# Samples dealt to the halves by twelves, count matmuls that write with a step, and a reordered prologue in a recommendation kernel

## What is computed

```python
x = _mlp(dense_x, bot, sigmoid_last=False)
pooled = jax.vmap(lambda tab, ix: jnp.take(tab, ix, axis=0).sum(axis=1))(tables, indices)
Tcat = jnp.concatenate([x[:, None, :], jnp.transpose(pooled, (1, 0, 2))], axis=1)
Z = jnp.einsum('bim,bjm->bij', Tcat, Tcat)
R = jnp.concatenate([x, Z[:, li, lj]], axis=1)      # li, lj: the lower triangle of 27 x 27
return _mlp(R, top, sigmoid_last=True)
```

## Time and profile before

| | |
|---|---|
| three runs, median (lowest to highest) | 2857.62 us (2854.86 to 2863.55) |
| profiled execution, its span | 2854.84 us, 2853.0 us |
| PE busy | 2743.9 us, 96% of the span |
| ACT busy | 2112.7 us, 74% |
| DVE busy | 1994.1 us, 70% |
| POOL busy | 1809.4 us, 63% |
| prologue, to the first sum matmul | 0 to 116 us |
| loop over the tables | 116 to about 2600 us |
| pairs of the 27 vectors and top MLP | the rest |

### The profile page before, as it was taken

How to read it: one execution, slowest core, us unless ns; L and a number is a source line. 1 busy time by engine, 2 the same in 40 slices (tenths; PEclk the granted TensorE clock), 3 DMA queues, 4 the chain that set the end, 5 groups by cost and what they waited for, 6 DMA issues and landing times.

```text
span 2853.0 us, 65593 instructions
## 1 busy us (share of the span) xinstructions
PE 2743.9 (96%) x24204; PEld 1305.1 (46%) x24204; DVE 1994.1 (70%) x3358; ACT 2112.7 (74%) x2496; POOL 1809.4 (63%) x1640
## 2 busy tenths in 40 slices
PE   5999999999999999999999999999999999999998
PEld 2344444444444444444444444444444444447963
DVE  4477787777877778787787877878778787753420
ACT  2778878788787887878878788787887878872431
POOL 3277777777777777777777777777777777400000
PEclk8999999999999999999999999999999999997579
DMA  2112122121221212212122121221212212007830
GB/s 69 62 32 76 28 78 75 32 76 28 78 75 32 76 29 78 74 32 77 31 76 74 32 77 30 76 74 32 77 30 77 74 32 74 20 26 111 137 85 0
DMA packets 173102, 167.99 MB, mean 59 GB/s; under 512 B 116104, under 2 KB 134328, under 8 KB 167476
## 3 DMA queue, kind: packets, MB, share of 16 engines
q1 hardware_dynamic: 121380, 110.94, 13.9%
q0 software_dynamic: 51200, 52.53, 9.4%
q10 hardware_dynamic: 272, 0.52, 0.1%
HBM read 143.83 MB, written 20.05 MB: 57 GB/s over the span
## 4 chain that ended last, share of the span: by engine, by line
PE 81%; ACT 11%; issue 3%; SPq 2%; DMA 1%; DVE 1%; ACTq 1%; DVEq 0%; POOL 0%; POOLq 0%
PE ps L693 58%; PE ps L674 14%; ACT counts L837 6%; PE ps L637 5%; ACT parts L799 3%; PE ps L764 3%; SPq L509 1%; ACT parts L806 1%; SPq L516 0%; ACT h_bot L850 0%; ACT pooled_sb L828 0%; SPq L532 0%; ACTq L834 0%; DMA pooled<-pooled_sb 0%; DMA look_in<-in_r_indices 0%
## 5 line engine op out<-in xcount | busy, mean ns | idle before, releaser
L611 POOL DMA_INDIRECT rows<-in_L_rec_tables,look x1600 | 1790.1, 1119 | 613.9 <-issue 453.7
L837 ACT CAST counts<-ps 128x792 int32<-128x792 f32 (+1 forms) x1848 | 1710.5, 983 | 471.7 <-PE ps L674 460.9
L693 PE MATMUL ps<-counts,parts 128*128 128x512 fp8e3 x8232 | 2019.2, 389 | 0.0
L693 PEld LDWEIGHTS ps<-counts,parts 128*128 128x128 f16 x8232 | 718.0, 96 | 912.1 <-issue 6.0
L1053 DVE TENSOR_TENSOR onehot_p<-iota_by_unit,place 128x1024 bf16<-128x1024 bf16 x924 | 637.4, 690 | 391.2 <-PE ps L674 363.2
L674 PEld LDWEIGHTS ps<-onehot_c,onehot_p 60*128 60x128 bf16 x14448 | 369.6, 95 | 479.9 <-ACT counts L837 272.2
L674 PE MATMUL ps<-onehot_c,onehot_p 60*128 60x99 bf16 x14448 | 521.6, 208 | 56.4 <-ACT counts L837 23.9
L1058 DVE TENSOR_TENSOR onehot_c<-column_c,weighted_s 128x792 bf16<-128x792 bf16 x924 | 520.4, 563 | 0.0
L1014 DVE SCALAR_TENSOR_TENSOR raw<-raw,coef_next,parts 128x896 f32<-128x896 f32 x147 | 168.8, 1148 | 60.0 <-ACT parts L799 59.9
L1087 DVE TENSOR_REDUCE rows<-rows 128x64 f32<-128x384 f32 (+1 forms) x240 | 189.7, 790 | 13.9 <-DVE pooled_sb L1064 13.9
L1064 DVE SCALAR_TENSOR_TENSOR pooled_sb<-ps,coef,pooled_sb 64x512 f32<-64x512 f32 x84 | 61.9, 737 | 145.8 <-ACT pooled_sb L828 145.8
(11 more groups left out here) (82 smaller groups left out, 524.8 us busy)
## 6 DMA issues: line engine op xcount, KB each, us to landing
raw<-in_L_rec_tables SPq DMA_DIRECT2D x21, 1792.0 KB
raw<-in_L_rec_tables SPq DMA_DIRECT2D x21, 1344.0 KB
rows<-in_L_rec_tables,look POOLq DMA_INDIRECT x1600
pooled<-pooled_sb SPq DMA_DIRECT2D x84, 128.0 KB, 2.3
slots<-pooled SPq DMA_DIRECT2D x30, 352.0 KB, 8.0
products<-zt SPq DMA_DIRECT2D x16, 351.0 KB
idx_raw<-in_r_indices SPq DMA_DIRECT2D x42, 79.7 KB
gathered<-bags_t SPq DMA_DIRECT2D x42, 64.0 KB
```

The costliest lines, as they stand in the source:

```text
L611: nc.gpsimd.indirect_dma_start(rows[:, s, l, :], None, rows_flat, bass.IndirectOffsetOnAxis(ap=look[:, c, s * PL + l:s * PL + l + 1].bitca ...
L693: mm = nc.tensor.matmul(acc[k % 2][:, 0:NB], parts[:, j, :], count_bytes[k % 2][:, j % COLS, 0:NB, j // COLS], start=(j == 0), stop=(j == ...
L837: nc.scalar.copy(counts[k % 2][:, :, u * UG * GS:(u * UG + g) * GS].rearrange("p c (g h s) -> p h g c s", h=HALVES, s=HS), unit_ps[unit_bu ...
```

## The change

1. **Samples.** A unit is 24 samples; the first 12 go to the lower half, the next 12 to the upper half (before, each group of 6 was split 3 and 3). The last unit of a block holds 8 samples, all in the lower half: 3 groups in place of 2, so 6 count matmuls in place of 4, 87 groups in place of 86. Its copy takes only the lower half.
2. **Count writes.** A count matmul writes its 99 results in 33 runs of 3, twelve elements apart, so that a half lies in PSUM as (column, 12 samples). The copy reads a half in one run as before, and writes runs of 12.
3. **Index blocks** of 88 groups in place of 86, in `idx_raw`, `idx_t`, `scratch`, `place`.
4. **Index loads.** Ten DMAs per table in place of three; ACT waits for 160 in place of 48.
5. **Prologue.** SP issues the four loads of input and weights first, before it waits for the constants, then the lookup indices, the index loads, the table and the small top loads. ACT issues the three biases. PE turns the weights before the indices. ACT takes the turned weights out of PSUM, a bank (up to four pieces) at a time in 8 copies, in place of DVE's 30; then it converts the indices.

```diff
+    US = UG * GS
+    UH = UG * HS
+    UNITS = -(-NB // US)
+    WHOLE = (UNITS - 1) * UG
+    LAST = NB - (UNITS - 1) * US
+    LAST_GROUPS = -(-LAST // HS)
+    GROUPS = WHOLE + LAST_GROUPS
+    TAIL = LAST - (LAST_GROUPS - 1) * HS
+    GPAD = UNITS * UG
...
             def load_indices(t):
-                cut = (GROUPS - 1) * GK
+                cut = (UNITS - 1) * US * L
                 for h in range(HALVES):
-                    sp.dma_start(idx_raw[0:GROUPS - 1, :, h * HP:h * HP + HK],
-                                 flat[:, 0:cut].rearrange("k (g h r) -> h g k r", h=HALVES, r=HK)[h]
-                                 ).then_inc(idx_loaded, 16)
+                    for x in range(UG):
+                        sp.dma_start(idx_raw[x:WHOLE:UG, :, h * HP:h * HP + HK],
+                                     flat[:, 0:cut].rearrange("k (u h x r) -> h x u k r", h=HALVES, x=UG, r=HK)[h, x]
+                                     ).then_inc(idx_loaded, 16)
+                full = (LAST_GROUPS - 1) * HK
+                sp.dma_start(idx_raw[WHOLE:GROUPS - 1, :, 0:HK],
+                             flat[:, cut:cut + full].rearrange("k (g r) -> g k r", r=HK)).then_inc(idx_loaded, 16)
...
-            sp.wait_ge(const_step, 4)
-            load_indices(0)
-                for dst, src in weight_loads:
+                for dst, src in weight_loads[:4]:
                     sp.dma_start(dst, src).then_inc(weights_in, 16)
+                load_lookups(0)
+                sp.wait_ge(const_step, 4)
+                load_indices(0)
                 for h in range(2):
                     load_table(rows_flat[0:SPAN * P, :], h)
...
-            load_lookups(0)
...
-                        last = nc.tensor.matmul(unit_ps[unit_buffer(k, u)][:, h, x * HC:(x + 1) * HC],
+                        last = nc.tensor.matmul(unit_ps[unit_buffer(k, u)][:, h, :].rearrange(
+                            "p (c x s) -> p x c s", x=UG, s=HS)[:, x, :, :],
...
-            turn_indices(0, first=True)
             pe.wait_ge(weights_in, 16 * len(weight_loads))
             turn(pe, turns, turned, unturned)
+            turn_indices(0, first=True)
...
-                act.wait_ge(idx_loaded, 48 * t + 48)
+                act.wait_ge(idx_loaded, 160 * t + 160)
...
+                halves = HALVES if u < UNITS - 1 else 1
                 nc.scalar.copy(
-                    counts[k % 2][:, :, u * UG * GS:(u * UG + g) * GS].rearrange(
-                        "p c (g h s) -> p h g c s", h=HALVES, s=HS),
-                    unit_ps[unit_buffer(k, u)][:, :, 0:g * HC].rearrange("p h (g c s) -> p h g c s", c=COLS, s=HS),
+                    counts[k % 2][:, :, u * US:u * US + halves * UH].rearrange("p c (h b) -> p h c b", b=UH),
+                    unit_ps[unit_buffer(k, u)][:, 0:halves, :].rearrange("p h (c b) -> p h c b", b=UH),
                 ).then_inc(counts_ready, 1)
...
+                for dst, src in weight_loads[4:]:
+                    act.dma_start(dst, src).then_inc(weights_in, 16)
...
+            for i, dst in enumerate(unturned_groups):
+                act.wait_ge(turned, i + 1)
+                m, items, kp = dst.shape
+                nc.scalar.copy(dst, banks[i % 4][0:m, 0:items * P].rearrange("p (k c) -> p k c", c=P)[:, :, 0:kp]
+                               ).then_inc(unturned, 1)
             convert_indices(0)
...
-            unturn(dve, turns, turned, unturned)
```

More of the change, by code:

```diff
@@ L66, in build @@
     BLOCKS = B // NB
-    GROUPS = -(-NB // GS)
-    TAIL = NB - (GROUPS - 1) * GS
     UG = 4
+    US = UG * GS
[7 more added lines that the diff above has]
+    GPAD = UNITS * UG
+    assert LAST <= UH
     LG = 2
     SUBS = UG // LG
-    UNITS = -(-GROUPS // UG)
     PAIRS = UNITS // 2
-    BPAD = GROUPS * GS
+    BPAD = (UNITS - 1) * US + UH
     CHUNKS = 7
@@ L187, in build @@
         b_top2c = sb(ctx, "b_top2c", [1, 1], F32)
-        idx_raw = sb(ctx, "idx_raw", [GROUPS, BLOCKS, P], I32)
+        idx_raw = sb(ctx, "idx_raw", [GPAD, BLOCKS, P], I32)
         idx_f = idx_raw[:, :, :].bitcast(F32)
@@ L222, in build @@
         weighted_s = sb(loop, "weighted_s", [P, UNITS * SUBS, HS, LG], BF16)
-        NI = BLOCKS * GROUPS
+        NI = BLOCKS * GPAD
         idx_t = sb(loop, "idx_t", [P, NI], F32)
         scratch = sb(loop, "scratch", [P, NI], F32)
-        NIP = NI + UNITS * UG - GROUPS
+        NIP = NI
         place_next = sb(loop, "place_next", [P, 3, NIP], BF16)
@@ L430, in load_indices @@
                 flat = indices[t].rearrange("b l -> (b l)").rearrange("(k r) -> k r", k=BLOCKS)
-                cut = (GROUPS - 1) * GK
+                cut = (UNITS - 1) * US * L
                 for h in range(HALVES):
-                    sp.dma_start(idx_raw[0:GROUPS - 1, :, h * HP:h * HP + HK],
-                                 flat[:, 0:cut].rearrange("k (g h r) -> h g k r", h=HALVES, r=HK)[h]
-                                 ).then_inc(idx_loaded, 16)
+                    for x in range(UG):
[5 more added lines that the diff above has]
+                             flat[:, cut:cut + full].rearrange("k (g r) -> g k r", r=HK)).then_inc(idx_loaded, 16)
                 sp.dma_start(idx_raw[GROUPS - 1:GROUPS, :, 0:TAIL * L],
-                             flat[:, cut:NB * L].rearrange("k (g r) -> g k r", g=1)).then_inc(idx_loaded, 16)
+                             flat[:, cut + full:NB * L].rearrange("k (g r) -> g k r", g=1)).then_inc(idx_loaded, 16)
             def load_lookups(n):
@@ L646, in turn_indices @@
                 for k in range(BLOCKS):
-                    last = nc.tensor.transpose(into[:, k * GROUPS:(k + 1) * GROUPS], idx_f[:, k, :],
-                                               ident[0:GROUPS, 0:GROUPS])
+                    last = nc.tensor.transpose(into[:, k * GPAD:(k + 1) * GPAD], idx_f[:, k, :],
+                                               ident[0:GPAD, 0:GPAD])
                 last.then_inc(idx_turned, 1)
@@ L809, in convert_indices @@
             def convert_indices(t):
-                act.wait_ge(idx_loaded, 48 * t + 48)
[L812 to L815, removed]
+                act.wait_ge(idx_loaded, 160 * t + 160)
+                nc.scalar.copy(idx_f[0:GROUPS, :, 0:TAIL * L], idx_raw[0:GROUPS, :, 0:TAIL * L]).then_inc(idx_converted, 1)
+                for groups, cols in ((GROUPS - 1, slice(TAIL * L, HK)), (WHOLE, slice(HP, HP + HK))):
+                    nc.scalar.copy(idx_f[0:groups, :, cols], idx_raw[0:groups, :, cols]).then_inc(idx_converted, 1)
             def copy_bags(n):
@@ L834, in unpack_unit @@
                 act.wait_ge(unit_counted, HALVES * n + HALVES)
-                g = len(units_of(u))
+                halves = HALVES if u < UNITS - 1 else 1
                 nc.scalar.copy(
-                    counts[k % 2][:, :, u * UG * GS:(u * UG + g) * GS].rearrange(
-                        "p c (g h s) -> p h g c s", h=HALVES, s=HS),
-                    unit_ps[unit_buffer(k, u)][:, :, 0:g * HC].rearrange("p h (g c s) -> p h g c s", c=COLS, s=HS),
+                    counts[k % 2][:, :, u * US:u * US + halves * UH].rearrange("p c (h b) -> p h c b", b=UH),
+                    unit_ps[unit_buffer(k, u)][:, 0:halves, :].rearrange("p h (c b) -> p h c b", b=UH),
                 ).then_inc(counts_ready, 1)
+            with nc.allow_non_contiguous_dma(reason="biases"):
+                for dst, src in weight_loads[4:]:
+                    act.dma_start(dst, src).then_inc(weights_in, 16)
+            unturned_groups = [xT[:, i * 4 * P:(i + 1) * 4 * P].rearrange("p (k c) -> p k c", c=P)
+                               for i in range(B // P // 4)]
+            unturned_groups.append(w_bot0T[:, :].rearrange("p (k c) -> p k c", c=P))
+            unturned_groups += [w_bot1T[:, :, m * P:(m + 1) * P] for m in range(NBOT[2] // P)]
+            unturned_groups.append(w_bot2T[:, :, :])
+            for i, dst in enumerate(unturned_groups):
[3 more added lines that the diff above has]
+                               ).then_inc(unturned, 1)
             convert_indices(0)
@@ L1032, in by_unit @@
                 def by_unit(i, count):
-                    return place[:, i, k * GROUPS:k * GROUPS + UNITS * UG].rearrange(
+                    return place[:, i, k * GPAD:(k + 1) * GPAD].rearrange(
                         "p (u a g) -> p u a g", a=1, g=LG).to_broadcast([P, UNITS * SUBS, count, LG])
@@ L1049, in onehot_pair @@
                 whole = [P, 2 * SUBS, P, LG]
-                g0 = k * GROUPS + 2 * UG * d
+                g0 = k * GPAD + 2 * UG * d
                 at = place[:, 0, g0:g0 + 2 * UG].rearrange("p (u a g) -> p u a g", a=1, g=LG).to_broadcast(whole)
```

## The result

The changed kernel takes 2881.14 us (median of four runs, 2879.65 to 2884.68) against 2856.91 us for the kernel before on the same chips: a ratio of 1.009, 95% interval 1.0078 to 1.0102. It is 24 us slower where 37 us faster was forecast. The profiled execution took 2879.65 us, its span is 2877.8 us.

The account below looks back on a forecast made before the run. PE was taken as the bound, with 114.8 us of its own work and 3.2 us of stalls per table. From 2854.8, - 16 - 24 + 4.2 + 0 = 2819, stated as 2820 us, range 2800 to 2925.

Parts of the forecast that it names:

- Part 1: Prologue: the new order starts the MLP 14.8 us earlier; taken as 16 us faster in all.
- Rival (d): Prologue: the reorder does less, the scale late for `make_hi`; 2 to 3 us lost; chance within the forecast's 0.48.
- Part 2: ACT's copies of 128x792: longer write runs save 100 ns each; 24 us faster, bounds 0 and 32.
- Rival (b): ACT's copies are no faster, with a free write: 2843 us; chance 0.07.
- Part 3: Count matmuls on PE: one more pair per block, 84 blocks x 0.05, 4.2 us slower.
- Part 4: Count matmuls on PE: the stepped write costs 0, with other ends at +37 and +237 us.
- rival (c): Count matmuls on PE: the stepped write is slow, over 0.45 ns per broken run; +140 or +237 us; chance 0.32.
- The room of 9 ns per pair: Count matmuls at full clock: a pair takes 0.050 us, its writing 0.041, so 9 ns are free.
- theory P: From the experiments, PE's count writes: results go in pairs of adjacent elements; a lone element costs two column times.
- The bound from ACT's runs: Count writes: 33 runs at ACT's 0.42 ns make 14, less 9 free: 5 ns per pair, +37 us.
- The other argument: Count matmuls starting at even and odd elements keep one pace, so writes not aligned to two elements cost nothing.
- Part 5: Index arithmetic on DVE and ten index issues on SP (some 5 us): covered, counted as nothing.

Follow-up runs that it names:

- contig_write: The changed kernel with count matmuls writing their 99 results in one run again and the copy writing runs of 3: 2841.42 us, ratio 0.996.
- read_runs: The changed kernel with contiguous count writes, the copy reading PSUM in runs of 3 and writing runs of 12: 2810.21 us, ratio 0.9853.

## Why the prediction was wrong, point by point

- **What bounds the kernel: right.** PE's pace and two stalls per table. The runs that changed the pace of the count matmuls, or one of the stalls, moved the time. But the size of the stall at the head of a table was read from one table, whose third phase of 31.06 is one of the shortest: over the 20 tables of that trace they run from 30.52 to 32.66, with a mean of 31.5.
- **Part 1, the prologue, -16: right in size, partly by luck.** Measured -14.6 in the trace. The order alone gave -17.3 as a kernel of its own, and -16.0 in its trace (first sum matmul at 100.20), with the MLP at 17.91. In the changed kernel the MLP starts at 20.13, not 18.8: eight index issues took 6.65, 0.83 each, where 0.42 was taken from two before. The blocks and loads cost 5.4 in the prologue (3.2 were counted for the loads), and the faster copies gave back 4 there (105.58 in `contig_write`, 101.19 in `read_runs`), which the forecast had not counted. The scale came at 39.95, not 38.5, and still ahead of its use at 42.76. Rival (d) didn't come.
- **Part 2, the copies, -24: right in kind, too small.** The copy fell to 822 ns, beyond the bound of 891 from the line through two other copies: 0.68 ns for each of 264 runs, not 0.42. The second phase lost its stall exactly; the one at the head stayed, a little shorter. The copy alone gave -31.3 in the old kernel and -31.2 between `contig_write` and `read_runs`. Of the latter pair's 33.2 between the spans 4.4 lie in the prologue and 28.4 in the loop: 1.0 per table in the second phase, as forecast, and 0.4 at the head (31.23 and 30.84 on average), where 0.2 was taken. Rival (b) falls.
- **Part 3, the extra pair, +4.2: right.** The first phase of the contiguous kernels with 87 groups is 28.60 against 28.55.
- **Part 4, the stepped write, 0: this is the step that failed.** It costs 0.083 us per group of eight pairs, 10.4 ns per pair and 77 us on 7392 pairs; 71 show between the loops of two kernels whose copies take the same time (`read_runs` and the changed one), since a slower PE waits about 4 us less at the heads of the tables. That is rival (c), which had 0.32 and decides from 6 ns on. Two arguments had led to zero. The room of 9 ns per pair is there only in part: 11 broken pairs, 4.6 ns by theory P, still cost 3, and 33 broken pairs are 14 ns and don't fit. The bound from ACT's runs had that same 14, by luck, and the forecast took the end below it; even the bound, 5 ns, is half of what was measured. The other argument was false: a contiguous write from an odd element breaks one pair in 50, and so its even pace says nothing of a write that breaks 33. What was missed is that a step has a price by the pairs that it breaks: at half clock that is all of it, at full clock a part of the price stays unexplained.
- **Part 5, the rest, at nothing: right in the loop alone.** Ten index issues there take 9.4 us and not some 5 (1109.31 to 1118.67), and still end before the next store at 1131.37. In the prologue they are not covered.
- **The sum.** Four kernels lead from before to after one part at a time, by their spans: the order of the prologue -20.6 (2853.0 to 2832.4), the blocks, loads and extra pairs +9.4 (2841.8), the copies -33.2 (2808.6), the step +69.2 (2877.8); together +24.8. The forecast had -16, +4.2, -24 and 0. About 5 of the 20.6 are no merit of the order (the medians say 17.3): the clock fell to 0.50 for some 3.4 us in each of four tables of the loop before (near 480, 599, 2255 and 2374 us; one is in the earlier trace rows), their third phases are 32.50 to 32.66, and the other traces of this chain have no such stretch in the loop. The range held the time, but its sign and its likeliest value were wrong.

## What to carry to other kernels

When a change moves a reordering from one engine to another, price it on the engine that sets the pace, and first ask whether the order of a copy's own loops does it for nothing: here the copy could read short runs from PSUM at no cost and write long ones. A resource that the trace never shows used in the new way has no price in the trace; if the engine is the bound, zero is the least safe guess, and one run of a cut-down variant settles it. A stall named for one engine can be a chain: follow it through the queue of the next engine, since moving one step there was worth 25 us, nearly as much as the copies. And read a stall from all its tables before you price it: one table can be among the cheapest.

## What the runs showed of the hardware that had not been expected

- At half clock a count matmul that writes runs of odd length pays one column time per run: 0.11 us per pair with 33 runs of 3, and 0.165 with 99 single elements, against 0.085 in one run. Runs of 4 are free there (0.08 for 96 columns).
- ScalarE's copy of 128x792 from PSUM takes 1001 ns when it writes SBUF in runs of 3, and 822 to 823 with runs of 12 or 24, whether it reads PSUM in one run or in runs of 3.
- At full clock runs of 9 cost 3 ns per pair, runs of 4 cost 5, and runs of 3 cost 10, twice what their broken pairs explain. This is open.
